# Layer 0 attention of a two-layer kernel: keys and values projected once, keys placed in three row groups when the bank is read

## The reference, cut to what matters

```python
q = x @ Wq.T          # 256 wide: 4 queries x 8 heads x 8
k = x @ Wk.T          # 64 wide: 8 heads x 8
v = x @ Wv.T          # 64 wide
scores = jnp.einsum('bsqhd,bthd->bqhst', qh, kh) * scale
probs = jax.nn.softmax(scores, axis=-1)
a_dot = jnp.einsum('bqhst,bthd->bsqhd', probs, vh)
a_mem = sigma_q @ memory / (sigma_q @ memory_norm)
out = a_dot * (1.0 - w) + a_mem * w
```

## Time and profile before

| what | value |
|---|---|
| median of 3 runs | 827.87 us (827.35 to 827.91) |
| the profiled execution, its own time | 828.4 us |
| its span, first to last instruction | 826.6 us |
| PE busy | 741.2 us, 90% of the span |
| PE weight loads busy | 638.3 us, 77% |
| DVE busy | 623.7 us, 75% |
| ACT busy | 468.0 us, 57% |
| POOL busy | 425.3 us, 51% |
| mean granted TensorE clock | 0.975 of full |

### The profile page before, as it was taken

The page is one execution under the profiler, slowest core; times in us unless marked ns, Lnnn a source line. Parts: engine busy times, 40 slices in busy tenths (PEclk is TensorE's granted clock), DMA queues, the critical chain, the costliest instruction groups (busy, mean ns, idle before and its releaser), DMA issues. The chain is left out here.

```text
span 826.6 us, 15174 instructions
## 1 busy us (share of the span) xinstructions
PE 741.2 (90%) x5602; PEld 638.3 (77%) x5602; DVE 623.7 (75%) x1095; ACT 468.0 (57%) x746; POOL 425.3 (51%) x369
## 2 busy tenths in 40 slices
PE   3267899999999999999999999999979899999873
PEld 3156778888888888888888888889857777877763
DVE  5989877787777777767768777767347698989965
ACT  4346646655665564665566557556676656565310
POOL 1334264354346658766634443544645485674732
PEclk9999999999999999999999999999979999999985
DMA  5111121121000110101100000011110000000000
GB/s 159 30 40 40 37 80 35 27 60 48 13 21 25 44 41 27 41 22 52 28 9 21 12 12 21 3 36 63 56 38 0 1 1 26 1 1 26 1 26 26
DMA packets 22109, 25.90 MB, mean 31 GB/s; under 512 B 4498, under 2 KB 17170, under 8 KB 22036
## 3 DMA queue, kind: packets, MB, share of 16 engines
q1 hardware_dynamic: 22036, 24.93, 10.6%
HBM read 14.83 MB, written 3.28 MB: 22 GB/s over the span
## 5 line engine op out<-in xcount | busy, mean ns | idle before, releaser
L652 DVE TENSOR_REDUCE neg_max<-s_pair 128x4 f32<-128x1024 f32 x127 | 155.0, 1220 | 74.1 <-PE s_pair L866 73.8
L474 ACT ACTIVATE probs<-t_pair 128x1024 f32<-128x1024 f32 x128 | 131.2, 1025 | 136.3 <-PE t_pair L891 136.0
L371 POOL TENSOR_TENSOR hid<-g,hid 128x512 f32<-128x512 f32 x64 | 82.2, 1284 | 176.2 <-DVE g L763 144.6
L365 POOL TENSOR_TENSOR hid_lo<-hid,hid_hi 128x512 fp32r<-128x512 f32 x64 | 85.6, 1338 | 82.7 <-ACT hid_hi L497 82.6
L866 PE MATMUL s_pair<-K,Q 96*128 96x256 f32 x508 | 85.4, 292 | 14.9 <-DVE neg_max L652 9.5
L866 PEld LDWEIGHTS s_pair<-K,Q 96*128 96x128 f32 x508 | 76.3, 196 | 23.6 <-issue 8.1
L891 PE MATMUL t_pair<-Q,K 104*128 104x512 f32 x256 | 86.5, 419 | 0.3 <-DMA Q<-max_parts 0.3
L933 PE MATMUL down<-hi,hid_hi 128*128 128x256 f32 x256 | 83.9, 328 | 0.8 <-POOL hid_lo L365 0.8
L933 PE MATMUL down<-lo,hid_hi 128*128 128x256 f32 x256 | 71.6, 279 | 0.0
L933 PE MATMUL down<-hi,hid_lo 128*128 128x256 f32 x256 | 71.2, 278 | 0.0
L906 PE MATMUL misc<-probs,V 128*32 128x256 f32 x1024 | 69.1, 387 | 1.8 <-DVE kc L608 1.0
(11 more groups left out here) (260 smaller groups left out, 1945.2 us busy)
## 6 DMA issues: line engine op xcount, KB each, us to landing
stage<-in_ternary SPq DMA_DIRECT2D x18, 256.0 KB, 2.8
Q<-q_hi SPq DMA_DIRECT2D x64, 64.0 KB, 2.0
stage<-in_scales SPq DMA_DIRECT2D x8, 384.0 KB, 3.4
X<-in_x SPq DMA_DIRECT2D x8, 256.0 KB, 3.9
Q<-q_lo SPq DMA_DIRECT2D x32, 64.0 KB, 2.0
Q<-max_parts SPq DMA_DIRECT2D x128, 4.0 KB
out<-X SPq DMA_DIRECT2D x8, 256.0 KB, 2.1
signs<-w_stage SPq DMA_DIRECT2D x9, 128.0 KB, 1.8
```

What stands on the lines that cost most here:

```text
L365: pool.tensor_tensor(hid_lo[:, m % 2, :, :].rearrange("p a n -> p (a n)"), hid[:, m % 2, :], hid_hi[:, m % 2, :, :].rearrange("p a n -> p ...
L371: pool.tensor_tensor(hid[:, m % 2, :], g[:, m % 2, :], hid[:, m % 2, :], ALU.mult).then_inc(S["hid_done"], 1)
L474: act.activation(probs[:, u % 2, th, :], t_pair[:], ACT.Exp, scale=SCALE).then_inc(S["probs_done"], 1)
L652: dve.tensor_reduce(neg_max[:, u % 2, 4 * jp:4 * jp + 4], score_banks(u, jp)[:].rearrange("p (s n) -> p s n", n=SEQ), AX_X, ALU.max, negat ...
```

## The change

The weights on the host are now simply [Wq, Wk, Wv], 384 columns, so `a_hi`, `a_lo` and `w_raw` shrink from 1024 to 768 elements in a row. Keys and values come from one product of 128 columns, six matmuls, into the first half of `misc`: rows 0 to 63 are the keys of the two quads, rows 64 to 127 the values. ACT now puts them in place with six copies of 32 rows by 256 elements: for each quad the keys to rows 0 to 31 and again to rows 32 to 63 of `kc`, and then the values of each quad to rows 96 to 127. DVE subtracts in two operations of 32 rows by 256, one for each quad, each once the quad's two key copies are there. The waits on the counters are adapted.

```diff
-        a_hi = sb("a_hi", [P, KC, 2 * D], F32R)
-        a_lo = sb("a_lo", [P, KC, 2 * D], F32R)
+        a_hi = sb("a_hi", [P, KC, D + P], F32R)
+        a_lo = sb("a_lo", [P, KC, D + P], F32R)
...
-                    pool.wait_ge(S["kc_lo_done"], b + 1)
+                    pool.wait_ge(S["kc_lo_done"], 2 * b + 2)
...
-                    act.activation(kc[0:KROWS, :, :], misc[0:KROWS, :].rearrange("p (c n) -> p c n", c=2), ACT.Copy).then_inc(S["kv_copied"], 1)
-                    act.activation(kc[KROWS:P, :, :].bitcast(F32), misc[KROWS:P, :].rearrange("p (c n) -> p c n", c=2), ACT.Copy).then_inc(S["kv_copied"], 1)
+                    e = QUAD * DH
+                    for quad in range(2):
+                        keys = misc[e * quad:e * quad + e, 0:SEQ]
+                        for part in range(2):
+                            act.activation(kc[e * part:e * part + e, quad, :], keys, ACT.Copy).then_inc(S["kv_copied"], 1)
+                    for quad in range(2):
+                        act.activation(kc[KROWS:P, quad, :].bitcast(F32), misc[2 * e + e * quad:3 * e + e * quad, 0:SEQ], ACT.Copy).then_inc(S["kv_copied"], 1)
...
-                    dve.wait_ge(S["kv_copied"], 2 * b + 1)
-                    lo = slice(2 * QUAD * DH, KROWS)
-                    dve.tensor_tensor(kc[lo, :, :], misc[lo, :].rearrange("p (c n) -> p c n", c=2), kc[lo, :, :].bitcast(F32),
-                                      ALU.subtract).then_inc(S["kc_lo_done"], 1)
+                    e = QUAD * DH
+                    for quad in range(2):
+                        same = slice(e * quad, e * quad + e)
+                        dve.wait_ge(S["kv_copied"], 6 * b + 2 * quad + 2)
+                        dve.tensor_tensor(kc[2 * e:KROWS, quad, :], misc[same, 0:SEQ], kc[same, quad, :].bitcast(F32),
+                                          ALU.subtract).then_inc(S["kc_lo_done"], 1)
...
-                    pe.wait_ge(S["kc_lo_done"], n + 1)
-                    pe.wait_ge(S["kv_copied"], 2 * n + 2)
+                    pe.wait_ge(S["kc_lo_done"], 2 * n + 2)
+                    pe.wait_ge(S["kv_copied"], 6 * n + 6)
...
-                    for c in range(2):
-                        mm = product(misc[:, SEQ * c:SEQ * c + SEQ], stationary(slice(D + P * c, D + P * c + P)), moving(b))
-                    mm.then_inc(S["kv_done"], 1)
+                    product(misc[:, 0:SEQ], stationary(slice(D, D + P)), moving(b)).then_inc(S["kv_done"], 1)
```

More of the change, by code:

```diff
@@ L159, in layer0 @@
         spare = probs[:].rearrange("p a b n -> p (a b n)")
-        w_raw = spare[:, 0:KC * 2 * D].rearrange("p (k n) -> p k n", k=KC)
+        w_raw = spare[:, 0:KC * (D + P)].rearrange("p (k n) -> p k n", k=KC)
         quarter = PAIRS_N * CW // 4
@@ L833, in step @@
                 elif kind == "kv":
-                    for c in range(2):
-                        mm = product(misc[:, SEQ * c:SEQ * c + SEQ], stationary(slice(D + P * c, D + P * c + P)), moving(b))
-                    mm.then_inc(S["kv_done"], 1)
+                    product(misc[:, 0:SEQ], stationary(slice(D, D + P)), moving(b)).then_inc(S["kv_done"], 1)
                 elif kind == "v":
-                    pe.wait_ge(S["kv_copied"], 2 * b + 2)
+                    pe.wait_ge(S["kv_copied"], 6 * b + 6)
                     for th in range(2):
@@ L1968, in layouts @@
     e = QUAD * DH
[L1969 to L1973, removed]
+    a["wqkv"] = np.concatenate([wq, wk, wv], axis=2)
     a["memory"] = f["L0_attn_memory"]
```

## The result

The changed kernel takes **822.75 us** (median of 4 runs, 821.29 to 823.19), the kernel before, run beside it, 827.89 (827.35 to 828.44). The ratio is 0.9939, with a 95% interval from 0.9925 to 0.9954: 5.1 us faster, where I forecast 1.85, and under my range. The profiled execution took 822.45 us with a span of 820.6, 6.0 less than before.

A forecast was written before the change was run, and what follows sets the result against it. PE was taken to bound the steady part of layer 0, DVE units 5 and 12. Steady units 1.75, less 0.4 for units 5 and 12, plus 0.5 prologue gave 1.85 us off 827.87: 826.0 us, range 824.6 to 828.3.

The forecast's parts named there:

- Six matmuls fewer, 0.72 us at full clock: PE, each batch: 6 x 0.12 us saved, a gain in five steady units, none in units 5 and 12.
- Six copies at 0.38 with a gap of 0.03: ACT, key and value copies: 0.41 us from start to start without overlap, 2.46 us in all.
- The full overlap: Rival: ACT's copies overlap, 0.28 us apart, and cost PE nothing; 2.8 us faster, 825.1 us; chance 0.28.
- The loss to ACT, 0.37: Steady units: PE waits for ACT's delayed `o_sb` copy, losing 0.37 of 0.72 us and keeping 0.35.
- 0.15 for release and weight load: Steady units: 0.15 us allowed between the end of ACT's `o_sb` copy and PE's L913.
- DVE's two subtractions, 0.3 where uncovered: Units 20, 44, 52: two operations take 0.91 us for 0.72; PE's 0.3 us wait is covered by ACT's loss.
- Losses of unit 5 and 12: PE waits longer for DVE's second subtraction there: 0.2 us lost in each, 0.4 together.
- The prologue: Start of the kernel: smaller weights shorten ACT and DVE operations; 0.5 us gained, bounds 0 and 1.0.
- I call that even: Prologue: PE's six matmuls less (0.72 or 1.44 us) against 1.2 us of extra copies ahead of ACT's tanh.
- an upper bound of 1.0: Prologue: gain of up to 1.0 us if POOL's spreading, which slows L597 to 1.60, starts earlier too.
- a rival for the clock: Unit 5: longer PE idling may bring another 1.2 GHz stretch, costing up to 1.7 us; 827.7 us; chance 0.12.
- The slower rival: ACT's copies cost 0.607 us each, 0.64 with the gap; 5.9 us slower in all, 833.8 us; chance 0.08.

The follow-up runs named there:

- a_mm12: The changed kernel with the six key and value matmuls run twice for batches 1 to 7, so PE has 12 again; 827.57 us, ratio 0.9998.
- a_v64: The changed kernel with the values copied in one 64-row operation and turned in two transposes, five ACT copies in place of six; 822.07 us, ratio 0.9923.
- a_wide: The changed kernel with projection weights as wide as before, 1024 elements a row, the last 256 unused; 822.05 us, ratio 0.9944.
- ctl_before: The kernel before, profiled once more with no edit; 826.53 us.
- b_pool_later: The kernel before with eight small memsets on POOL ahead of the spreading of quad 1 in the prologue; 825.43 us, ratio 0.9976.

## Why the prediction was wrong

The sign was right, the size was not: 5.1 us where the sum said 1.85, and below the range.

- *Six matmuls fewer, 0.72 us at full clock*: right. a_mm12 gives 0.71 in each unit.
- *Six copies at 0.38 with a gap of 0.03*: right, 0.375 each and 0.40 from start to start. The full overlap did not come: here copies whose rows change from one to the next don't overlap. That only this makes the difference is a reading, not shown by itself. By the Trainium skill, page "ScalarE: Activation LUTs", section "What ACT_TABLE_LOAD costs", with its overlap of 93 ns, it would have been 0.28 from start to start, an estimate from that and the measured 0.375; the trace doesn't agree.
- *The loss to ACT, 0.37*: measured 0.26. L918 began 0.05 after the `o_sb` copy ended (299.29 and 299.34), where I had allowed 0.15 for release and weight load. That term was a little too large: five times 0.1 us. Most of the loss, 0.22, is already there at L911, which waits for the sixth copy.
- *DVE's two subtractions, 0.3 where uncovered*: right, 0.25 in unit 20 by a_v64. Losses of unit 5 and 12: 0.17 and 0.13 against 0.2 each.
- *The prologue*, the step that failed. The narrow weights took 0.22 and 0.27 off their two operations, as forecast (what arrives of it varies, see a_wide). "I call that even" held for what it compared: the copies of "kv" began 1.28 sooner behind the start of `q_hi` (1.71 us for 2.99, matmuls at the slow pace in both), tanh 1.17 later behind them, and with the 0.42 that `q_hi` came earlier L597 started 0.53 earlier. But it compared the wrong path. The end of L597 is set by POOL's spreading, which starts as soon as the second subtraction is done, and the subtraction ended only 0.71 later behind the start of the copies (2.02 for 1.31). I had named this, as an upper bound of 1.0, and taken half; it came in full (-0.98 at the end of L597). Against ctl_before, where the twelve matmuls ran at the fast pace (copies 1.75 us behind `q_hi`), there is no such gain. And the collision of POOL's second spreading with L712 I had not looked at at all: a row of 2.35 us, where an operation of its shape alone takes 0.95, was in the trace. b_pool_later shows that it is worth 1.36 us, and that half a microsecond of order decides.
- *Units 5 and 6*: I had a rival for the clock, with the opposite sign. A low stretch did follow the wait in unit 5 (1.92 us in place of 1.03), but the longer wait is not shown to be its cause, as four traces of the kernel before waited 2.55 to 2.62 us without one. Its price was hidden by the wait for POOL behind it, and the one of the kernel before, behind that wait, which was not hidden, fell away. The price of 1.7 us was right in size (the turning of unit 6 comes 1.70 later), and the wait behind it gave most of it back. How often it happens in either kernel is open.
- *The slower rival* (copies at 0.6 us) is refuted by the rows of L437 and L439.

The parts that came back in all three traces of either kernel, 1.36 from the order, 5 x 0.45 and the -0.13 of unit 12, make 3.5 of the 5.1 us; the rest are the two that vary. The range failed for the same reason as the sum: it took its bounds in the prologue from a shift of all the work by some tenths, not from an operation whose duration depends on who comes first.

## What to carry to other kernels

Ahead of a sum of shifts, list the operations whose duration differs between executions of the same shape, here DVE's 0.95 to 2.35 us beside a POOL operation: each is a place where a shift of 0.1 us is worth over a microsecond, in either direction, and where a small delay of the engine that isn't on the path can be a gain. Look too at how far each of the two hangs on the same work: here one moved by 0.99 and the other by 0.54. When operations are moved to another engine, price start to start, and then look for the engine behind it: here DVE was 0.02 us behind ACT's price in three of five units (8.88 and 8.90 us). Here a lower clock cost only what no later wait hid. And before a part of a difference is put down to a change, see whether it moves between two executions of the same kernel.

## What the runs showed of the hardware

- The subtraction of 128x768 on DVE in the prologue, with both inputs in SBUF, took 0.90 to 0.96 us or 2.24 to 2.70, and POOL's spreading 1.89 or 2.5 to 3.1, by which of the two was ahead, with leads of 0.10 to 0.12 us deciding.
- ACT copies of 32 rows by 256 elements, to other rows than they come from, took 0.375 us each, like a copy of 128 rows (0.382); a copy of 64 rows in a_v64 0.38.
- One program's executions differed by up to 1.5 us between the same two points of its timeline, as the stretches at 1.2 GHz fell ahead of or behind a wait of PE, or fell away.
- The same twelve matmuls of "kv" in the prologue ran at 0.43 or 0.24 us a pair, with 1.00 in the column of the granted clock both times, and moved the first turning by 1.8 us (before and ctl_before).
